# Attention with exponential gates: the key side of the decay exponents moved into spare rows of each chunk

## The reference, cut to what matters

```python
ig = (gi @ igate_w.T + igate_b).transpose(0, 2, 1)
fg = (gi @ fgate_w.T + fgate_b).transpose(0, 2, 1)
log_f = jax.nn.log_sigmoid(fg)
cs = jnp.cumsum(log_f, axis=-1)
diff = cs[..., :, None] - cs[..., None, :]
log_D = jnp.where(tril, diff, -inf) + ig[..., None, :]
max_log_D = jnp.max(log_D, axis=-1, keepdims=True)
D = jnp.exp(log_D - max_log_D)
C = qk * D
normalizer = jnp.maximum(jnp.abs(C.sum(-1, keepdims=True)), jnp.exp(-max_log_D))
h = jnp.einsum('bhst,bhtd->bhsd', C / (normalizer + EPS), vh)
...
hn = (h - mean) / jnp.sqrt(var + LN_EPS) * out_w
x = x + jnp.tanh(g_xattn[0]) * hn
```

## Time and profile before

| what | value |
| --- | --- |
| median of 3 runs | 3075.43 us (3074.34 to 3090.6) |
| the profiled execution | 3074.24 us, its span 3072.5 us |
| TensorE busy in the span | 2964.4 us (96%) |
| VectorE | 1832.6 us (60%) |
| ScalarE | 1138.2 us (37%) |
| GpSimd | 1057.8 us (34%) |
| mean granted clock of TensorE | 0.986 |

### The profile page before, as it was taken

How to read it: one execution, slowest core, us unless ns; L and a number is a source line. 1 busy time by engine, 2 the same in 40 slices (tenths; PEclk the granted TensorE clock), 3 DMA queues, 4 the chain that set the end, 5 groups by cost and what they waited for, 6 DMA issues and landing times.

```text
span 3072.5 us, 60746 instructions
## 1 busy us (share of the span) xinstructions
PE 2964.4 (96%) x24708; PEld 2398.2 (78%) x24708; DVE 1832.6 (60%) x5124; ACT 1138.2 (37%) x2025; POOL 1057.8 (34%) x1028
## 2 busy tenths in 40 slices
PE   6999999999997599999999999999999999999998
PEld 5888888888886477777777777787787777778886
DVE  6999998999998645354454444445435444444322
ACT  5778787877886311121121121122112112112110
POOL 4767687777766211111112111121112111121111
PEclk9999999999998799999999999999999999999999
DMA  3243434434342422231242131232123214222121
GB/s 129 84 166 113 167 135 144 158 121 167 130 149 104 137 42 35 37 99 31 44 100 47 37 79 34 37 95 62 31 37 88 45 31 110 37 49 58 35 37 23
DMA packets 140062, 250.68 MB, mean 82 GB/s; under 512 B 31457, under 2 KB 31457, under 8 KB 139785
## 3 DMA queue, kind: packets, MB, share of 16 engines
q1 hardware_dynamic: 105784, 170.80, 16.5%
q0 software_dynamic: 28672, 67.65, 12.5%
q10 hardware_dynamic: 5328, 8.36, 0.9%
HBM read 137.23 MB, written 101.19 MB: 78 GB/s over the span
## 4 chain that ended last, share of the span: by engine, by line
PE 63%; DMA 2%; DVE 1%; issue 0%; ACT 0%; POOL 0%; ACTq 0%; DVEq 0%; POOLq 0%
PE DN L1710 31%; PE UP L1684 29%; PE TT L1657 2%; DMA w_raw<-in_L_ffn_W_down 2%; DVE c_hit L1380 0%; DVE down_lo L1246 0%; PE c_bank L1373 0%; ACT z L1629 0%; PE c_bank L1357 0%; DVE c_hit L1401 0%; DVE c_within L1396 0%; ACT down_hi L1240 0%; POOL out_x L1604 0%; DVE mid_lo L1742 0%; DVE c_gained L1433 0%
## 5 line engine op out<-in xcount | busy, mean ns | idle before, releaser
L1604 POOL DMA_INDIRECT out_x<-y,slots x128 | 202.0, 1578 | 1640.5 <-DVE y L1764 1640.5
L1710 PE MATMUL DN<-down_hi,mid_hi 128*128 128x512 f32 x1408 | 579.2, 411 | 0.0
L1629 ACT ACTIVATE z<-UP,bup 128x512 f32<-128x512 f32 (+1 forms) x352 | 240.8, 686 | 853.8 <-PE UP L1684 836.9
L1684 PE MATMUL UP<-xT_hi,up_hi 128*128 128x512 f32 (+1 forms) x1408 | 553.1, 393 | 1.9 <-DVE xT_lo L1721 0.9
L1684 PE MATMUL UP<-xT_hi,up_lo 128*128 128x512 f32 (+1 forms) x1408 | 554.8, 394 | 0.0
L1684 PE MATMUL UP<-xT_lo,up_hi 128*128 128x512 f32 (+1 forms) x1408 | 551.3, 392 | 0.0
L1710 PE MATMUL DN<-down_hi,mid_lo 128*128 128x512 f32 x1280 | 505.1, 395 | 0.0
L1710 PE MATMUL DN<-down_lo,mid_hi 128*128 128x512 f32 x1280 | 504.9, 394 | 0.0
L1740 DVE CAST mid_hi<-z 128x512 fp32r<-128x512 f32 (+1 forms) x352 | 151.1, 429 | 484.3 <-ACT z L1629 484.3
L1613 ACT ACTIVATE xT_hi<-TT 128x512 fp32r<-128x512 f32 x126 | 75.1, 597 | 702.9 <-PE TT L1657 682.9
L1684 PEld LDWEIGHTS UP<-xT_hi,up_hi 128*128 128x128 f32 (+1 forms) x1408 | 259.8, 185 | 68.5 <-ACT z L1629 4.5
(11 more groups left out here) (263 smaller groups left out, 5005.3 us busy)
## 6 DMA issues: line engine op xcount, KB each, us to landing
xs<-in_x SPq DMA_DIRECT2D x32, 1024.0 KB, 8.3
kraw<-in_ctx SPq DMA_DIRECT2D x32, 1024.0 KB, 5.7
out_x<-xs SPq DMA_DIRECT2D x32, 1024.0 KB, 12.7
rows_scratch<-xfb SPq DMA_DIRECT2D x32, 1024.0 KB, 10.8
w_raw<-in_L_ffn_W_down SPq DMA_DIRECT2D x40, 512.0 KB, 4.4
w_raw<-in_L_ffn_W_up SPq DMA_DIRECT2D x16, 682.5 KB, 4.1
mid_hi<-mid_hi ACTq DMA_DIRECT2D x32, 86.0 KB
mid_lo<-mid_hi ACTq DMA_DIRECT2D x32, 84.0 KB
```

What stands on the lines that cost most here:

```text
L1604: pool.indirect_dma_start(out_rows, bass.IndirectOffsetOnAxis(ap=slots[:, m:m + 1], axis=0), y[:, t, :], None, compute_op=ALU.add).then_in ...
L1629: act.activation(z[0:r, k % 2, :], UP[k % 3][0:r, :], ACT.Silu, bias=bup[0:r, e // 2, f:f + 1]).then_inc(s["z"], 1)
L1684: mm = pe.matmul(UP[k % 3][0:r, :], weights.up[wa][:, c, f * P:f * P + r], xT[xa][:, c, :], start=first, stop=(c == CH - 1 and wa == 1))
L1710: mm = pe.matmul(DN[m % 2][:, :], lhs, rhs, start=first, stop=(f == FCH - 1 and lhs is parts[-1][0]))
```

## The change

The key side no longer has products of its own. Each chunk's 16 unused rows of `peaks` are set to one, once, among the constants. SP copies the 16 used rows of `rise` in each chunk into the 16 spare rows of a new tile `lift`, with four DMAs a batch; the other 16 rows of `lift` are set to -1 once. GpSimd's `split_climb` works on `lift` and then makes `climbs`, which for each head holds `climb` on that head's rows and zero on the others: two products with a spread `ofhead`, for heads 0 and 1 first and then for the other six. `decays` uses `climbs` in the place of `sel`, so that one product of 256 columns adds the key side and takes off the peaks; the two products with `pick` are gone. GpSimd does `split_climb` after the first two of the four `weigh_columns`. `sel` and `pick` are no longer made; `ofhead`, `lift_lows` and the ones in `peaks` are.

```diff
+                def lift_rise(b):
+                    wait_taken(sp, "shift", b, 0)
+                    if b:
+                        sp.wait_ge(s["rp"], b)
+                    for j in range(TILES):
+                        at = QD * j
+                        sp.dma_start(lift[at + 2 * HEADS:at + QD, :], rise[at:at + 2 * HEADS, :]).then_inc(s["lifted"], 16)
...
                     store_probabilities(i - 7)
+                    if live(i - 1):
+                        lift_rise(i - 1)
...
+                step(pool.memset(lift[:, :], -1.0))
...
-                        if row % QD < 2 * HEADS:
-                            step(pool.affine_select(out=heads[:, :], in_=heads[:, :], compare_op=ALU.not_equal, fill=1.0,
+                        for one in (heads, ofhead) if row % QD < 2 * HEADS else (ofhead,):
+                            step(pool.affine_select(out=one[:, :], in_=one[:, :], compare_op=ALU.not_equal, fill=1.0,
                                                     base=-row, pattern=[[-1, HEADS]], channel_multiplier=1))
...
-                    step(pool.tensor_scalar(sel[:, :, :], spread(heads[:, :], 2, P), -1.0, None, ALU.mult))
...
+                    for n in range(2):
+                        step(pool.tensor_copy(peaks[:, n, :], C[:, 5, :]))
...
                 def split_climb(b):
 
-                    wait_taken(pool, "shift", b, 0)
-                    if b >= 2:
-                        pool.wait_ge(s["ee"], 2 * PAIRS * (b - 1))
-                    step(pool.tensor_scalar(climb_low[:, :], rise[:, :], lows[:, 0:1], None, ALU.mult))
-                    pool.tensor_tensor(climb[:, b % 2, :], rise[:, :], climb_low[:, :].bitcast(FP32), ALU.subtract).then_inc(s["rp"], 1)
+                    pool.wait_ge(s["lifted"], 16 * TILES * (b + 1))
+                    step(pool.tensor_scalar(climb_low[:, :], lift[:, :], lift_lows[:, 0:1], None, ALU.mult))
+                    pool.tensor_tensor(climb[:, :], lift[:, :], climb_low[:, :].bitcast(FP32), ALU.subtract).then_inc(s["rp"], 1)
                     pool.wait_ge(s["rp"], b + 1)
+                    if b:
+                        pool.wait_ge(s["ee"], 2 * PAIRS * b)
+                    for h, n in ((0, 2), (2, HEADS - 2)):
+                        pool.tensor_tensor(climbs[:, h:h + n, :], spread(climb[:, :].bitcast(FP32), 1, n), spread(ofhead[:, h:h + n], 2, P), ALU.mult)\
+                            .then_inc(s["cl"], 1)
+                    pool.wait_ge(s["cl"], 2 * (b + 1))
...
+                    if live(b3):
+                        weigh_columns(step, pool, b3, slice(0, 2))
                     if live(b1):
                         split_climb(b1)
                     if live(b3):
-                        weigh_columns(step, pool, b3, slice(0, TILES))
+                        weigh_columns(step, pool, b3, slice(2, TILES))
...
-                    if p == 0:
-                        pe.wait_ge(s["rp"], b + 1)
-                    for a, r in ((0, top), (1, end)):
-                        ones_of = pick[r, p, :, :].rearrange("k a j -> k (a j)")
-                        pe.matmul(EX[:, a, :], climb[r, b % 2, :], spread(ones_of, 2, P), start=False, stop=False, skip_group_check=True)
+                    if p < 2:
+                        pe.wait_ge(s["cl"], 2 * b + p + 1)
...
-                            mm = pe.matmul(EX[:, a, par * 2 * P:(par + 1) * 2 * P], sel[r, 2 * p + par, :], peaks[r, b % 2, half],
+                            mm = pe.matmul(EX[:, a, par * 2 * P:(par + 1) * 2 * P], climbs[r, 2 * p + par, :], peaks[r, b % 2, half],
...
                     if b >= 1:
-                        dve.wait_ge(s["rp"], b)
+                        dve.wait_ge(s["lifted"], 16 * TILES * b)
...
-                        rows = slice(QD * j, QD * j + QD)
+                        rows = slice(QD * j, QD * j + 2 * HEADS)
```

More of the change, by code:

```diff
@@ L119, in attention @@
         lg = sb("lg", [P, P]); gsum = sb("gsum", [P, P]); shift = sb("shift", [P, P])
-        sel = sb("sel", [P, HEADS, P], FP32R); selP = sb("selP", [P, HEADS, DH], FP32R)
+        climbs = sb("climbs", [P, HEADS, P], FP32R); ofhead = sb("ofhead", [P, HEADS]); selP = sb("selP", [P, HEADS, DH], FP32R)
         peaks = sb("peaks", [P, 2, SEQ], FP32R); inner = sb("inner", [P, 2, SEQ - P], FP32R); held = sb("held", [P, 2, P], FP32R)
@@ L127, in attention @@
         maskneg = sb("maskneg", [P, SEQ], BF16); maskswap = sb("maskswap", [P, SEQ], BF16)
-        climb = sb("climb", [P, 2, P], FP32R); climb_low = sb("climb_low", [P, P], FP32R)
-        pick = sb("pick", [P, PAIRS, 2, 2], FP32R)
+        climb = sb("climb", [P, P], FP32R); climb_low = sb("climb_low", [P, P], FP32R)
+        lift = sb("lift", [P, P]); lift_lows = sb("lift_lows", [P, TILES])
         gW = sb("gW", [P, 2 * CH, QD])
@@ L149, in attention @@
                  "ee dd qk cc af an sq sr x2 x2v lex smx hs vc uv "
[L150 removed]
+                 "ldg rp lifted cl x2t xf2v dchain achain pchain prep1 prep2 prep3").split()
         s = {n: sem("a_" + n) for n in names}
@@ L325, in constants @@
-                    step(pool.tensor_tensor(lows[:, 0:2], lows[:, 0:2], lows[:, 2:4], ALU.add))
-                    step(pool.tensor_tensor(lows[:, 0:1], lows[:, 0:1], lows[:, 1:2], ALU.add))
+                    for rows, first in ((lows, HEADS), (lift_lows, 3 * HEADS)):
+                        step(pool.memset(rows[:, :], 1.0))
+                        step(pool.affine_select(out=rows[:, :], in_=rows[:, :], compare_op=ALU.is_ge, fill=0.0,
+                                                base=-first, pattern=[[-QD, TILES]], channel_multiplier=1))
+                        step(pool.affine_select(out=rows[:, :], in_=rows[:, :], compare_op=ALU.is_ge, fill=0.0,
+                                                base=first + HEADS - 1, pattern=[[QD, TILES]], channel_multiplier=-1))
+                        step(pool.tensor_tensor(rows[:, 0:2], rows[:, 0:2], rows[:, 2:4], ALU.add))
+                        step(pool.tensor_tensor(rows[:, 0:1], rows[:, 0:1], rows[:, 1:2], ALU.add))
@@ new lines, in constants @@
+                    ones_of = C[:, 5, :].rearrange("p (j t) -> p j t", j=TILES)
+                    step(pool.memset(ones_of, 1.0))
+                    step(pool.affine_select(out=ones_of, in_=ones_of, compare_op=ALU.is_ge, fill=0.0,
+                                            base=-2 * HEADS, pattern=[[-QD, TILES], [0, P]], channel_multiplier=1))
+                    step(pool.affine_select(out=ones_of, in_=ones_of, compare_op=ALU.is_ge, fill=0.0,
+                                            base=QD - 1, pattern=[[QD, TILES], [0, P]], channel_multiplier=-1))
@@ L334, in constants @@
                                             base=QD - 1, pattern=[[QD, TILES]], channel_multiplier=-1))
-                    step(pool.tensor_tensor(wt[:, 0:2], own[:, 0:2], own[:, 2:4], ALU.add))
-                    step(pool.tensor_tensor(pick[:, :, :, :].rearrange("k p a j -> k (p a) j"), spread(heads[:, :], 2, 2),
-                                            spread(wt[:, 0:2], 1, HEADS), ALU.mult))
                     step(pool.memset(unseen[:, :], 0.0))
@@ L885, in _ @@
                 ins.then_inc(s["clear"], 1)
-                for t in (gW[:, :, :], peaks[:, :, :].bitcast(FP32), inner[:, :, :].bitcast(FP32)):
+                for t in (gW[:, :, :], inner[:, :, :].bitcast(FP32)):
                     step(dve.memset(t, 0.0))
```

6 lines of the change are left out of this document (1 added, 5 removed).

## The result

The changed kernel takes 3141.05 us (median of 4 runs, 3137.59 to 3145.39) against 3078.42 for the kernel before (4 runs beside them): ratio 1.0206, 95% interval 1.0187 to 1.0224. It is slower by 63 us. The forecast was 3105, in a range of 3078 to 3130: the direction was right, the size less than half of what came. The profiled execution took 3145.39 us, with a span of 3143.7.

The account below looks back on a forecast made before the run. A ring through VectorE's `nn`, GpSimd's `uv` and TensorE's `chunk_state` and scores was taken to set the period; 30 periods x 0.98 = 29.4, + 2 - 4 + 3 = +30.4 on 3074.24 gave 3105 us, range 3078 to 3130.

Parts of the forecast that it names:

- The ring: Loop cycle `nn`, GpSimd to third `uv`, `chunk_state`, scores of pair 1, VectorE to `nn`; slack 0.95 us a period.
- Climbs on GpSimd: Two `climbs` products a batch ahead of `uv` on GpSimd, taken at 2.02 us, 2.2 us with two waits.
- Removed products: The two 512-column products dropped from each `decays` on TensorE, taken to give back 0.32 us per `decays`.
- Disturbances: Mean loop period 0.52 us over the undisturbed one, 13.5 us in all; 4 us taken back, 3 added for half-clock stretches.
- Nothing else stands behind the copies on SP until the next key load, which waits for `chunk_state` anyway: SP's queue: the four copies from `rise` to `lift` delay nothing there and land 0.5 to 0.8 us early, no cost.
- The ring's 0.98: Added us per loop period: 2.20 on GpSimd less slack 0.95, less 0.32 removed, with 0.05 for the hand-over.
- the forecast's +30.4: Whole kernel: 30 periods x 0.98 = 29.4, + 2 start, - 4 disturbances, + 3 half-clock stretches.
- The sum: Whole-kernel total: +30.4 us on the profiled execution's 3074.24 us, giving 3105 us.
- Rival 1: TensorE's clock falls in every period after the stalls for climbs and at `chunk_state`: about 3120, up to 3135; 10%.
- Rival 2: Copies to `lift` come late behind bulk stores on the same queue, 0.5 us a period: about 3120; 8%.
- Rival 3: Faster: GpSimd not in the ring, if `climbs` cost under 1.1 us; VectorE's 0.66 us waits go: 3057; 10%.
- Rival 4: No measurable change: ring stretches by 0.98 but all 13.5 us of disturbances vanish in new waits: about 3090; 12%.

Follow-up runs that it names:

- e2: Changed kernel with SP issuing a round's row load ahead of its key load: 3114.70 us, ratio 1.0118 to the kernel before.
- e4: Kernel before the change with the row load ahead of the key load on SP: 3066.26 us, ratio 0.9962.
- e13: e2 with head selector and period-before exponents replacing climbs and peaks, so TensorE does not wait for climbs (decay exponents left out): 3108.55 us.
- e15: e12 with the masks of pair 3 laid down three times, just ahead of TensorE's wait for `rise`: 3109.48 us.
- e18: e15 with VectorE's `head_variances` (the instructions on `top`) behind the moments of the new rows: 3074.77 us.
- e7: e2 with the six-head climbs product moved on GpSimd from in front of `uv` to behind it: 3109.12 us.
- e8: e2 with `uv` put behind the third of the four `weigh_columns` on GpSimd: 3112.00 us.
- e5: Changed kernel with the scores of pair 0 ahead of its decays on TensorE: 3138.39 us, ratio 1.0189.
- e12: e13 with the split and both climbs products at the end of GpSimd's round, so nothing waits for them: 3140.39 us.
- e21: e2 with split and climbs behind the first `weigh_columns`, `uv` behind the third, `top` behind the moments of new rows: 3093.96 us.
- e20: e8 without TensorE's climbs wait (decay exponents left out), pair 3's masks laid three times, `top` behind the moments of new rows: 3075.59 us.

## Why the prediction was right in direction and wrong in size

The ring was there. Per clean period, e2 against e4 (and the round above against the earlier trace rows):

| link | forecast | measured |
| --- | --- | --- |
| `weigh_heads` to the end of `uv` | +2.20 | 14.31 to 16.55: +2.24 |
| end of `uv` to the C product of pair 1 | -0.95 - 0.32 + 0.05 = -1.22 | 4.57 to 3.50: -1.07 |
| C product to the moments of new rows | 0 | 5.61 to 5.89: +0.28 |
| moments to `nn` | 0 | 4.52 to 4.52: 0 |
| period | +0.98 | 29.16 to 30.61: +1.45 |

- **Climbs on GpSimd** at 2.02 us: measured 2.04. The estimate from the Trainium skill (GPSIMD Engine Reference, sections 3.1 and 4.1), 2.25 us for 1024 columns, was too high here.
- **Removed products.** "I use" 0.32 us per `decays` was too much: the spacing from the masks to the next instruction fell only from 0.99 to 0.77 us (medians), by 0.22. "The 256-column products stay as they are" did not hold: they average 329 ns where those with `sel` averaged 279. The first two of the four, which now stand right behind the masks, take 382, the last two 276. The operand `climbs` is not the cause, since e13 has `selP` and `inner` in this place and the same mean:

```profile
L779 PE MATMUL EX<-inner,selP 64*128 64x256 f32 x156 | 19.6, 329 | 0.0
```

- **VectorE** was taken to run on unchanged. But GpSimd's round is 2.2 us longer and its end no longer lies ahead of `top`. In the kernel before (GpSimd's and VectorE's order of time below) centring ended at 490.16 and `top` began at 490.74; in the round above it ended at 553.76 and `top` had begun at 553.32. This is the 0.28: the four instructions on `top` take 1.08 us in e2 and 0.8 in e4. e15 against e18 (1.75 us of VectorE a period, one edit) shows what the collision costs when it is deeper, and with the times of `top` in e7 and e8 it is a reason why an earlier `uv` was worth so little: it brings VectorE forward against GpSimd's centring.
- **The step that failed** is "Disturbances", with the sentence on SP's queue ("Nothing else stands behind the copies on SP until the next key load, which waits for `chunk_state` anyway"). I took 4 us back for them and added 3 for the clock. Behind that key load stands the row load, and VectorE was already waiting for it in 13 rounds of the loop. In the round of the kernel before that is shown below, VectorE read the new rows 8.9 us after the key load's issue (483.31, where the stretch of the earlier trace rows begins, to 492.23). In the round of the changed kernel above it is ready for them 8.6 us after it (546.57 to 555.16), but they land after 9.4 (9.0 from the row load's own issue). The medians of the loop's rounds say the same: VectorE is ready after 8.6 us where it was 9.0, and the rows land after 9.4 where it was 9.2. Two small pushes made a wait in 25 rounds. The late VectorE then holds `rise`, for which TensorE waits, and the clock falls; in e2 this wait of TensorE is gone, too. e2 and e4 price the whole: 26.4 us now, 12.2 before, so 14.2 more instead of 1 less.
- **The ring's 0.98** was mis-sized beside it: 1.45 measured, by the three links above. Of the 32.2 us between the forecast's +30.4 and the measured +62.6, the disturbances are 15.2, the ring is 14.1, and 2.9 is the rest.
- **The sum**, re-made: 30 periods x 1.45 = 43.5, + 14.2, + 4.9 for the rest = 62.6 measured (the rest is what remains: e2 - e4 = 48.4, less 43.5). In the rest lie the start, where the first products come at 37.20 and not at 33.71 (+3.5, forecast +2), and the late copies.
- **Rival 1**, the clock, came true in half of the periods, but from another wait than it named. Its place was the stall for the climbs and `chunk_state`; e5 takes the wait for the climbs off the list and keeps the falls, e13 has 1.9 us of idle time at `chunk_state` in a period on average and no fall. In the changed kernel 12 of the 14 falls stand right behind a wait for `rise` (1.19 + 0.22 us just ahead of 438.52), and the two others do not. The Trainium skill's rule (TensorE: Matmul & The Clock Gate, "A second HAM failure mode"), that frequent small gaps between groups of matmuls can make the clock go to and fro, agrees with e12, where it fell in 24 periods one after another, and with e15, which filled that gap and had 2 such stretches; it does not tell why e13, with gaps in each period, had none.
- **Rival 2**, late copies, is real but small: GpSimd waits for them 3.3 us in 6 rounds of the changed kernel's loop. The copies are issued over 2.42 us, not 1.3, and land in 1.8, not 2.3 to 2.6. It costs more only in e21 (19.3 us in 15 rounds).
- **Rival 3** is out: its condition was `climbs` under 1.1 us, and they take 2.04. Even in e18, where nothing waits for GpSimd's added work, 3075 is above the 3066 of e4, which has the same row load; how much of that the two mask passes of e18 cost was not run. (Its sum, 3074 - 20 + 2, is 3056 and not 3057; nothing hangs on it.) **Rival 4** is out, since the disturbances grew.

The rows of the kernel before for `top` and the row load:

```profile
486.11 4.05 POOL L369 TENSOR_TENSOR vc<-kraw,hs 128x512 f32<-128x512 f32 x4
```

```profile
490.74 0.21 DVE L944 TENSOR_TENSOR top<-nsb,tm 128x32 f32<-128x32 f32 x1
...
492.23 1.27 DVE L903 BATCH_NORM_STATS2 st<-xs 128x6 f32<-128x512 f32 x2
```

What stays open: why a 256-column product right behind the masks is some 0.1 us longer, why the load of new rows lands 0.2 us later, and what sets the 0.2 us a period that e20 keeps over e4 (the two mask passes may be part of it).

## What to carry to other kernels

Several rings can have almost the same length. When cutting one gains a tenth of what was cut, look for what became late next, and cut them together: here 1.45 us a period was held by GpSimd's `uv`, by the climbs into pair 0 and by a collision of two engines, and the clock took back part of what was won. None of the cuts that were made alone on e2 (e7, e8, e13) was worth over 0.2; moving `top` alone, or the mask passes alone, was not run. Before pricing a longer link, look up every wait that is already there in part of the rounds, as the row load was: it has no slack left and takes the first push. The order of two loads that are issued together is worth a try on its own: it gave 12 us to a kernel that was not otherwise touched.

## What the runs showed of the hardware

- VectorE's small instructions on `top` take 0.18 to 0.21 us alone and up to 0.96 to 0.97 beside GpSimd instructions of about 1.0 us. The moments of four tiles are not touched: 2.46 us at 550.41 in the changed kernel, beside the centring, and 2.47 at 556.01, behind it.
- A GpSimd product with a spread operand takes 612 and 1469 ns for 256 and 768 columns, near the rate that the 512-column rows gave:

```profile
L410 POOL TENSOR_TENSOR climbs<-climb,ofhead 128x768 fp32r<-128x768 f32 x32 | 47.0, 1469 | 0.0
L410 POOL TENSOR_TENSOR climbs<-climb,ofhead 128x256 fp32r<-128x256 f32 x32 | 19.6, 612 | 2.5
```

- 0.43 us of TensorE work laid ahead of a wait of 1.0 us (24.6 us in 24 periods) took 119.5 us of half-clock down to 6.8 (e12, e15), while idle pieces of 1.28, 0.33 and 0.33 us behind `uv` in e13 left the clock at 1.00:

```profile
526.37 0.69 PE L796 MATMUL T<-uv,kraw 128*64 128x65 f32 x16 [1.28 <-POOL uv L397]
527.38 0.69 PE L796 MATMUL QK<-uv,kraw 128*64 128x65 f32 x16 [0.33 <-POOL uv L397]
528.39 0.69 PE L796 MATMUL QK<-uv,kraw 128*64 128x65 f32 x16 [0.33 <-POOL uv L397]
```
